# Eight token tiles of an attention output projection: fp32 products against three fp32r products, on one Trainium2 core

## The chip, the cores and the metric

The kernel runs on one core of one Trainium2 (trn2) chip. The metric is the device time of one launch in microseconds (us). The kernel before took 902.72 us, the median of three runs (902.1 to 905.22). The engines are TensorE (PE in the profile; PEld is its load of the stationary operand), VectorE (DVE), ScalarE (ACT), GpSimd (POOL) and SyncE (SP); SP, ACT and POOL also issue DMAs.

## The reference, cut to what matters

The input x has 2 batches of 1024 tokens of 512 numbers, 2048 tokens in all.

```
xn  = layernorm(x)
qkv = xn @ w_attn + b_attn                  # 16 heads of 32
q, k = rope(q), rope(k)
attn = softmax(causal(q @ k.T)) * 512**-0.5
o    = attn @ v                             # back to 2048 x 512
out  = x + (o @ w_proj + b_proj) + moe(xn)  # 8 experts, top 2
```

The change is about `o @ w_proj`: a product of 2048 x 512 by 512 x 512, and only about its first 1024 tokens (batch 0).

## The kernel before, in words

The kernel has three stages, and each is a block that ends only when all engines have done their part: `project_qkv` (layernorm, q, k, v, router), `attend` (attention and the output product of batch 0) and `experts` (the output product of batch 1, then the experts over 39 slot tiles).

**Attention.** Work goes in 16 rounds (`ROUNDS`), numbered n = 0 to 15. Round n handles one pair of heads of one batch, the set n mod 4. Each of the four sets has its own stack of queries, `q_st[i]`, and of keys, `k_st[i]`, of 128 partitions by 2048 fp32r numbers. Sets 0 and 1 belong to batch 0, sets 2 and 3 to batch 1. So `q_st[0]`, `k_st[0]`, `q_st[1]`, `k_st[1]` are last read in rounds 12 and 13, `q_st[2]` and `k_st[2]` in round 14, and only set 3 is used in round 15. A round has 12 steps (`NS`); a step has two score products (L1467), two exponentials on ACT (L1340) and two products with the values (L1487). In 8 steps of the 12, POOL sets the masked half of the probabilities to zero (L1285), and TensorE's products with the values wait for that (semaphore `masked`). The row maxima are computed a round and a half ahead (`LEAD` = 36 of 24 units per round): score products of their own on TensorE (L1444) and reductions on DVE (L1370, L1374). So DVE's part of the rounds ends in the middle of round 14.

**Scaling.** After every two rounds the sums of the exponentials of a "span" (one group of 8 heads of one batch: 8 spans, `SPANS`) go to memory and back through SP's queue: `load_totals` (L1178), DVE's reciprocal (`share`, L1392), `store_shares` (L1182), `spread_shares` (L1190), and then POOL multiplies that part of `o_t` (`scale_span`, L1270). The seventh span, the last of batch 0, is scaled in round 15. The eighth span belongs to batch 1; its `share` stands in DVE's program right after the first of the eight additions described next.

**The output product of batch 0** (`EARLY` = 8 tiles of 128 tokens). When its rounds are done, TensorE waits for the first seven spans (`scaled`) and for all banks, and then runs for each tile four fp32 products of 128 x 128 by 128 x 512, added up in one PSUM bank (L1529). The eight tiles use six banks in turn (`proj_banks`), so tiles 6 and 7 wait for DVE to be done with tiles 0 and 1 (`res_done`). DVE adds the residual (L1418) and SP stores the tile (L1220). POOL meanwhile adds the bias to the residual of the second half (`add_bias`, L1259, eight of them).

**The hand-over.** The block ends when SP has issued the last store and all engines are done. In `experts`, POOL then builds an identity matrix (L785, L787), TensorE waits for it and starts the output product of batch 1 (L990, the same fp32 form), and the expert tiles follow.

The fp32r form is already used elsewhere: `project_qkv` computes q and k as hi*hi + hi*lo + lo*hi (L535 to L537, 512 columns each), with a high part rounded to fp32r and a low part that is the difference. Differences of the same kind on DVE are L357 and L890; L351 is an addition of the same shape from SBUF to SBUF.

Of the kernel before, what the change touches and what calls it, by code (L numbers as in the profile page):

```python
# [18 lines left out]
ALU = mybir.AluOpType  # L19
# [3 lines left out]
P = 128  # L23
B, S, D = 2, 1024, 512
# [9 lines left out]
NG = H // HG  # L34
# [6 lines left out]
PAIR = 2  # L41
# [3 lines left out]
EARLY = S // P  # L45
# [4 lines left out]
def as_f32(ap):  # L50

    return ap.bitcast(F32)
# [946 lines left out]
def attend(nc, keep, scratch, x, w_proj, b_proj):  # L999
# [3 lines left out]
    ROUNDS = NG * SETS  # L1003
# [12 lines left out]
    NS = len(steps)  # L1016
# [9 lines left out]
    SPANS = NG * B  # L1026
# [24 lines left out]
    with ctx:  # L1051
        m = Memory(nc, ctx)
        q_st = [m.sbuf(f"q_stack{i}", [P, PAIR, S], F32R) for i in range(SETS)]
        k_st = [m.sbuf(f"k_stack{i}", [P, PAIR, S], F32R) for i in range(SETS)]
# [15 lines left out]
        o_t = keep["o_t"]  # L1070
# [5 lines left out]
        mb = [m.psum(f"maxima{r}", [P, CH]) for r in range(RING)]  # L1076

        proj_banks = scores_t + mb

        scattered, tags_in = m.sem("scattered"), m.sem("tags_in")  # L1080
        w_proj_in = m.sem("w_proj_in")
# [9 lines left out]
        st_full = m.sem("st_full")  # L1091
# [6 lines left out]
        scaled = m.sem("o_scaled")  # L1098
        bp_in, res_in, biased = m.sem("bp_early_in"), [m.sem(f"res_in{i}") for i in range(NT // 2)], m.sem("biased_early")
        proj_full, res_done = m.sem("proj_early_full"), m.sem("res_early_done")  # L1100
        acc_rows = scratch["acc"][0:T, :].rearrange("(a p) (g t) -> a p g t", p=P, t=P)
        QK_LOADS = 6
        OUTS = 2 * PAIR
# [256 lines left out]
        def _(dve):  # L1360
# [26 lines left out]
            def share(span):  # L1387

                dve.wait_ge(totals_in, 16 * (span + 1))
                if span:  # L1390
                    dve.wait_ge(shares_out, 16 * span)
                nc.vector.reciprocal(shares[:], totals[:]).then_inc(shares_done, 1)  # L1392

            def ahead(slot):

                if unit_at(slot) is not None:
                    n, u = unit_at(slot)
                    unit(n, u)
                    if u == NU - 1:
                        join(n)  # L1400
                if turn_at(slot - LOW_LAG) is not None:
                    row_low(turn_at(slot - LOW_LAG))
# [5 lines left out]
            for n in range(ROUNDS):  # L1408
                for u in range(NU):
                    ahead(n * NU + u)  # L1410
                    if u == (NB - 1) * PER - 1 and n % PAIRS == 0 and n:
                        share(n // PAIRS - 1)
                if n == 1:
                    route_owners(dve)
            for a in range(EARLY):
                dve.wait_ge(proj_full, a + 1)
                dve.wait_ge(biased, a + 1)
                nc.vector.tensor_tensor(o_t[:, :, a * P:(a + 1) * P], proj_banks[a % len(proj_banks)][:].rearrange("p (g t) -> p g t", t=P),  # L1418
                                        res[:, a, :].rearrange("p (g t) -> p g t", t=P), ALU.add).then_inc(res_done, 1)
                if a == 0:  # L1420
                    share(SPANS - 1)

        @block.tensor
        def _(pe):
# [83 lines left out]
            for n in range(ROUNDS):  # L1508
                for s in range(NB):
                    for x in range(BATCH * PAIR):  # L1510
                        k, h = (s + 1) * BATCH + x // PAIR, x % PAIR
# [13 lines left out]
            for a in range(EARLY):  # L1525
                if a >= len(proj_banks):
                    pe.wait_ge(res_done, a - len(proj_banks) + 1)
                for g in range(NG):
                    last = nc.tensor.matmul(proj_banks[a % len(proj_banks)][:], o_t[:, g, a * P:(a + 1) * P], keep["w_proj"][:, g, :],  # L1529
                                            start=(g == 0), stop=(g == NG - 1))  # L1530
                last.then_inc(proj_full, 1)


# [72 lines left out]
```

## Time and profile before

| what | value |
|---|---|
| median of the runs | 902.72 us |
| the profiled execution: its own time, its span | 906.29 us, 904.6 us |
| granted TensorE clock over the span | 0.954 |
| busy over the span: PE, DVE, ACT, POOL | 91%, 57%, 44%, 28% |
| output product of batch 0 on TensorE (L1529) | from 533.15 to 560.9 us |
| its records, additions on DVE | 64 records of 32 products, 8 additions |

The span is the time from the first to the last instruction of the profiled execution; 1.7 us lie around it. That execution took 3.6 us more than the median. Each fp32 product shows as two matmul records. A record's duration is longer than the distance between two starts, since products are pipelined: the distance between starts is what one costs in a row of many. The granted clock of 1.00 is 2.4 GHz and 0.50 is 1.2 GHz; values between are mixtures of the two over a stretch.

### The profile page before, as it was taken

What the parts mean: (1) busy time and instruction counts of PE and PEld (TensorE: products, weight loads), DVE (VectorE), ACT (ScalarE), POOL (GpSimd) and SP (SyncE); (2) the same over time, 40 slices, a digit from 0 to 9 for tenths busy, and PEclk for the clock granted to TensorE, in tenths of its full rate; (3) what the DMA queues carried; (4) which work ended last, traced back from release to release, by engine and by line L of the source; (5) the groups of instructions that cost most, each with busy time, mean ns of one, the idle gap of its engine ahead of it and who ended that gap; (6) DMA issues with size and microseconds to landing.
All of it is one profiled execution on the core that took longest, in us unless ns stands there. A gap on an engine that the chain in (4) does not pass through costs nothing. (4 is left out here: it accounts for less than half of the span.)

```text
span 904.6 us, 13761 instructions
## 1 busy us (share of the span) xinstructions
PE 820.4 (91%) x3973; PEld 559.8 (62%) x3974; DVE 515.3 (57%) x1334; ACT 394.8 (44%) x779; POOL 249.4 (28%) x314
## 2 busy tenths in 40 slices
PE   3889999569989999999999998979999999999990
PEld 3768989435445555555555443458778777787860
DVE  5992543395466667666666401166666666666640
ACT  3231231104445556555555630046666655556630
POOL 3782000134132424323233251002223223222220
PEclk9899999856899999999999999999999999999995
DMA  9386695894445755597671014843663664633327
GB/s 323 144 254 198 201 320 182 269 236 144 145 148 144 229 140 160 134 234 188 180 180 56 15 57 113 278 151 70 165 160 75 168 173 73 172 71 70 70 35 208
DMA packets 80477, 143.21 MB, mean 158 GB/s; under 512 B 16688, under 2 KB 30512, under 8 KB 80368
## 3 DMA queue, kind: packets, MB, share of 16 engines
q10 hardware_dynamic: 29056, 58.28, 23.8%
q1 hardware_dynamic: 43200, 65.72, 23.6%
q0 software_dynamic: 8176, 18.65, 9.8%
q8 instruction: 22, 0.36, 0.2%
q14 instruction: 23, 0.19, 0.1%
HBM read 81.21 MB, written 61.15 MB: 157 GB/s over the span
## 5 line engine op out<-in xcount | busy, mean ns | idle before, releaser
L1340 ACT ACTIVATE probs<-scores_t 128x512 f32<-128x512 f32 (+3 forms) x384 | 163.8, 492 | 148.7 <-PE scores_t L1467 136.9
L890 DVE TENSOR_TENSOR w_lo<-w,w_hi 128x704 fp32r<-128x704 f32 x156 | 131.7, 885 | 91.1 <-ACT w_hi L822 83.7
L1444 PE MATMUL maxima<-k_stack,q_stack 96*128 96x512 f32 (+3 forms) x384 | 142.2, 391 | 15.0 <-DMA q_stack<-qk_hi 9.0
L1487 PE MATMUL o_acc<-probs,v_ones 128*64 128x512 f32 (+3 forms) x768 | 149.9, 513 | 0.0
L1467 PE MATMUL scores_t<-q_stack,k_stack 98*128 98x512 f32 (+3 forms) x384 | 138.5, 386 | 7.2 <-DMA q_stack<-row_lo 5.1
L1374 DVE TENSOR_REDUCE mx<-maxima 128x1 f32<-128x512 f32 x128 | 88.2, 689 | 89.5 <-PE maxima L1444 89.3
L1370 DVE CUSTOM_DVE_ANT_0 masked_scores<-maxima,mask_m 128x128 f32<-128x128 f32 (+3 forms) x256 | 121.5, 485 | 23.8 <-PE maxima L1444 20.7
L822 ACT CAST w_hi<-w 128x704 fp32r x156 | 114.1, 783 | 34.2 <-issue 33.5
L935 PE MATMUL gu<-w_hi,rows_hi 128*128 128x352 f32 x312 | 119.7, 384 | 5.3 <-DVE rows_lo L883 4.0
L1467 PEld LDWEIGHTS scores_t<-q_stack,k_stack 98*128 98x128 f32 x384 | 73.6, 194 | 70.0 <-issue 42.7
L953 PE MATMUL down<-w,hidden_t 128*128 (+1 forms) x234 | 108.0, 597 | 0.8 <-DVE hidden_t L877 0.8
L936 PE MATMUL gu<-w_lo,rows_hi 128*128 128x352 f32 x312 | 101.5, 325 | 0.0
L937 PE MATMUL gu<-w_hi,rows_lo 128*128 128x352 f32 x312 | 101.3, 325 | 0.0
L1444 PEld LDWEIGHTS maxima<-k_stack,q_stack 96*128 96x128 f32 x384 | 77.5, 204 | 35.8 <-issue 9.5
L1285 POOL TENSOR_SCALAR_AFFINE_SELECT probs<-probs 128x256 f32<-128x256 f32 x120 | 48.4, 406 | 145.1 <-ACT probs L1340 143.5
L1487 PEld LDWEIGHTS o_acc<-probs,v_ones 128*64 128x64 f32 x768 | 47.8, 139 | 64.5 <-issue 39.6
L834 ACT ACTIVATE y<-down,tags 128x512 f32<-128x512 f32 x39 | 26.9, 689 | 107.7 <-PE down L953 58.7
L800 POOL COPY row_index<-tags 128x1 f32 (+1 forms) x39 | 8.7, 223 | 234.2 <-ACT y L834 173.3
L935 PEld LDWEIGHTS gu<-w_hi,rows_hi 128*128 128x128 f32 x312 | 59.1, 189 | 15.4 <-DVE w_lo L890 7.7
L801 POOL DMA_INDIRECT acc<-y,row_index x39 | 63.3, 1624 | 16.8 <-issue 15.4
L953 PEld LDWEIGHTS down<-w,hidden_t 128*128 128x128 f32 (+1 forms) x234 | 42.1, 190 | 39.8 <-issue 38.3
L280 ACT ACTIVATE st_hi<-bank,small 128x512 fp32r<-128x512 f32 x32 | 21.9, 687 | 101.8 <-PE bank L537 101.8
(158 smaller groups left out, 1168.9 us busy)
## 6 DMA issues: line engine op xcount, KB each, us to landing
w<-in_w_t SPq DMA_DIRECT2D x8, 1408.0 KB, 6.6
routed<-blank_row ACTq DMA_DIRECT2D x20, 514.0 KB, 6.5
rows<-routed ACTq DMA_DIRECT2D x39, 256.0 KB, 3.5
qk_hi<-st_hi SPq DMA_DIRECT2D x32, 256.0 KB, 4.7
qk_lo<-st_lo SPq DMA_DIRECT2D x32, 256.0 KB, 6.0
q_stack<-qk_hi ACTq DMA_DIRECT2D x32, 256.0 KB, 4.1
k_stack<-qk_hi ACTq DMA_DIRECT2D x26, 256.0 KB, 4.7
v_all<-o_t SPq DMA_DIRECT2D x4, 1536.0 KB, 5.7
```

The source lines that it names most:

```text
L822: nc.scalar.copy(w1_hi[r][:, k, :], w1_rows(slot, k)).then_inc(w1_hi_done, 1)
L890: nc.vector.tensor_tensor(w1_lo[r][:, k, :], w1_rows(slot, k), as_f32(w1_hi[r][:, k, :]), ALU.subtract).then_inc(w1_done, 1)
L935: nc.tensor.matmul(out, hi, w1_hi[r][:, k, cols], start=(k == 0), stop=False)
L936: nc.tensor.matmul(out, hi, w1_lo[r][:, k, cols], start=False, stop=False)
L937: last = nc.tensor.matmul(out, lo, w1_hi[r][:, k, cols], start=False, stop=(k == DK - 1))
L953: last = nc.tensor.matmul(down[r][:], hidden_t[r][0:n, k, :], w2[0:n, bass.ds(e, 1), k, :].rearrange("p o n -> p (o n)"), start=(k == 0), ...
L1340: nc.scalar.activation(probs[:, k % PR, h, 0:w], scores_t[e % RING][:, 0:w], ACT.Exp).then_inc(exp_done, 1)
L1370: nc.vector.tensor_tensor_reduce(out=masked_scores[bank][:, 0:w], in0=scores, in1=mask_m[:, CH - w:CH], scale=1.0, scalar=NEG, op0=ALU.add ...
L1374: nc.vector.tensor_reduce(to, scores, AX.X, ALU.max).then_inc(m_free, 1)
L1444: nc.tensor.matmul(mb[at % RING][:, 0:w], q_st[i][0:3 * HD, h, t * P:(t + 1) * P], k_st[i][0:3 * HD, h, c * CH:c * CH + w], start=True, st ...
L1467: last = nc.tensor.matmul(out[:, 0:w], k_st[i][0:STACK, h, j * P:(j + 1) * P], q_st[i][0:STACK, h, t0:t0 + w], start=True, stop=not diag)
L1487: last = nc.tensor.matmul(o_acc[c][2 * HD * h:2 * HD * (h + 1), CH - w:CH], v_st[i][:, j, h:h + 2, :].rearrange("p o d -> p (o d)"), probs ...
```

## The change

Each fp32 product of the eight tiles becomes three fp32r products, and DVE makes the four operands: the high and low part of `w_proj` (4 pieces of 512 columns) and the high and low part of `o_t` (8 tiles of 4 x 128 columns). The parts of `w_proj` go into `q_st[2]` and `k_st[2]`, as soon as all score products of rounds 0 to 14 are done (`st_full`). The parts of `o_t` go into the stacks of sets 0 and 1 (tile a into set a // 4, high in the query stack, low in the key stack), as soon as seven spans are scaled. All 24 new DVE instructions stand ahead of the eight additions in DVE's program. TensorE waits for each tile's low part, and for the four pieces of the weights.

```diff
+        wp_hi, wp_lo = (t[2][:].rearrange("p h (g n) -> p (h g) n", n=D) for t in (q_st, k_st))
+        def projected(stacks, a):
+            page = stacks[a // NG][:].rearrange("p h (x n) -> p (h x) n", n=D)
+            return page[:, a % NG, :]
...
+            def output_weights(g):
+                if g == 0:
+                    dve.wait_ge(w_proj_in, 16)
+                    dve.wait_ge(st_full, (ROUNDS - 1) * NS * PAIR)
+                nc.vector.tensor_copy(wp_hi[:, g, :], keep["w_proj"][:, g, :]).then_inc(wp_hi_done, 1)
+                dve.wait_ge(wp_hi_done, g + 1)
+                nc.vector.tensor_tensor(wp_lo[:, g, :], keep["w_proj"][:, g, :], as_f32(wp_hi[:, g, :]), ALU.subtract).then_inc(wp_done, 1)
+            def projected_parts(a):
+                tile = o_t[:, :, a * P:(a + 1) * P]
+                hi, lo = (projected(t, a).rearrange("p (g t) -> p g t", t=P) for t in (q_st, k_st))
+                if a == 0:
+                    dve.wait_ge(scaled, SPANS - 1)
+                nc.vector.tensor_copy(hi, tile).then_inc(o_hi_done, 1)
+                dve.wait_ge(o_hi_done, a + 1)
+                nc.vector.tensor_tensor(lo, tile, as_f32(hi), ALU.subtract).then_inc(o_done, 1)
+            for g in range(NG):
+                output_weights(g)
+            for a in range(EARLY):
+                projected_parts(a)
             for a in range(EARLY):
                 dve.wait_ge(proj_full, a + 1)
                 dve.wait_ge(biased, a + 1)
...
+                bank = proj_banks[a % len(proj_banks)]
+                pe.wait_ge(o_done, a + 1)
+                pe.wait_ge(wp_done, NG)
                 for g in range(NG):
-                    last = nc.tensor.matmul(proj_banks[a % len(proj_banks)][:], o_t[:, g, a * P:(a + 1) * P], keep["w_proj"][:, g, :],
-                                            start=(g == 0), stop=(g == NG - 1))
+                    hi, lo = (projected(t, a)[:, g * P:(g + 1) * P] for t in (q_st, k_st))
+                    nc.tensor.matmul(bank[:], hi, wp_hi[:, g, :], start=(g == 0), stop=False)
+                    nc.tensor.matmul(bank[:], hi, wp_lo[:, g, :], start=False, stop=False)
+                    last = nc.tensor.matmul(bank[:], lo, wp_hi[:, g, :], start=False, stop=(g == NG - 1))
                 last.then_inc(proj_full, 1)
```

## Rows read from the trace of the kernel before

**Rows 1.** Page, busy time of the engines and the chain that ended last.

```profile
PE 820.4 (91%) x3973; PEld 559.8 (62%) x3974; DVE 515.3 (57%) x1334; ACT 394.8 (44%) x779; POOL 249.4 (28%) x314
PE 34%; DVE 1%; issue 1%; POOL 0%; ACT 0%; ACTq 0%; DVEq 0%; POOLq 0%
```

**Rows 2.** Busy time by stretch; then granted clock, DMA share, GB/s.

```profile
core 0: us, PE busy (x) PEld busy (x) DVE busy (x) ACT busy (x) POOL busy (x), PEclk, DMA share, GB/s
88.20:93.75 5.55, 5.55 (x26) 4.46 (x24) 2.47 (x11) 1.49 (x3) 0.00 (x0) 1.00 1.07 267
533.15:560.90 27.75, 27.74 (x66) 12.09 (x64) 5.19 (x8) 0.58 (x1) 10.00 (x8) 1.00 0.31 92
560.90:563.50 2.60, 0.00 (x0) 0.00 (x0) 0.69 (x1) 0.00 (x0) 0.54 (x3) 1.00 0.26 74
591.70:595.70 4.00, 0.00 (x0) 0.00 (x0) 3.97 (x6) 1.85 (x4) 0.00 (x0) 1.00 0.80 279
595.70:600.00 4.30, 4.27 (x18) 4.20 (x19) 1.70 (x2) 1.96 (x4) 0.00 (x0) 0.60 0.21 63
```

**Rows 3.** VectorE in order of time, 508 to 563 us: start, duration, instruction, idle before.

```profile
511.07 0.33 DVE L1392 RECIPROCAL shares<-totals 128x32 f32<-128x32 f32 x1
536.89 0.69 DVE L1418 TENSOR_TENSOR o_t<-scores_t,x_rows 128x512 f32<-128x512 f32 x1 [25.50 <-PE scores_t L1529]
538.83 0.35 DVE L1392 RECIPROCAL shares<-totals 128x32 f32<-128x32 f32 x1 [1.25 <-DMA totals<-totals_all]
...
560.92 0.69 DVE L1418 TENSOR_TENSOR o_t<-scores_t,x_rows 128x512 f32<-128x512 f32 x1 [2.74 <-PE scores_t L1529]
```

**Rows 4.** TensorE in order of time, 88 to 94 us: first and last of 24 products.

```profile
88.20 0.40 PE L535 MATMUL bank<-xt_hi,w_hi 128*128 128x512 f32 x1
...
93.52 0.39 PE L537 MATMUL bank<-xt_hi,w_lo 128*128 128x512 f32 x1
```

**Rows 5.** TensorE in order of time, end of rounds 14 and 15.

```profile
512.51 0.56 PE L1467 MATMUL scores_t<-q_stack,k_stack 98*128 98x256 f32 x3
513.37 0.33 PE L1467 MATMUL scores_t<-q_stack,k_stack 98*128 98x128 f32 x1 [0.30 <-ACT probs L1340]
...
518.76 1.73 PE L1487 MATMUL o_acc<-probs,v_ones 128*64 128x512 f32 x8
...
530.85 2.37 PE L1487 MATMUL o_acc<-probs,v_ones 128*64 128x512 f32 x16
533.15 1.12 PE L1529 MATMUL scores_t<-w_proj,o_t 128*128 128x512 f32 x2
```

**Rows 6.** GpSimd in order of time, 516 to 563 us.

```profile
516.98 0.41 POOL L1285 TENSOR_SCALAR_AFFINE_SELECT probs<-probs 128x256 f32<-128x256 f32 x1 [2.49 <-ACT probs L1340]
517.74 0.41 POOL L1285 TENSOR_SCALAR_AFFINE_SELECT probs<-probs 128x256 f32<-128x256 f32 x1 [0.36 <-ACT probs L1340]
...
525.72 2.38 POOL L1270 TENSOR_TENSOR o_t<-o_t,share_rows 128x1024 f32<-128x1024 f32 x1 [6.10 <-DMA share_rows<-shares_all]
...
530.88 0.82 POOL L1285 TENSOR_SCALAR_AFFINE_SELECT probs<-probs 128x256 f32<-128x256 f32 x2 [1.72 <-ACT probs L1340]
531.67 9.13 POOL L1259 TENSOR_TENSOR x_rows<-x_rows,bp_early 128x512 f32<-128x512 f32 x8
544.69 2.35 POOL L1270 TENSOR_TENSOR o_t<-o_t,share_rows 128x1024 f32<-128x1024 f32 x1 [3.88 <-DMA share_rows<-shares_all]
562.81 0.21 POOL L785 MEMSET ident<- 128x128 f32 x1 [15.78 <-POOLq L1051]
```

**Rows 7.** Single lines: ns min/median/max, first and last start.

```profile
L435 DVE TENSOR_SCALAR x_rows<-x_rows,mean_var,rstd x2: 542/542/543, 12.6 to 13.1; 128x512 f32<-128x512 f32 x2
L357 DVE TENSOR_TENSOR w_lo<-w_raw,w_hi x8: 680/1090/1361, 27.7 to 46.6; 128x512 fp32r<-128x512 f32 x8
L226 POOL TENSOR_SCALAR x_rows<-x_rows,mean_var,rstd x12: 2070/2074/3512, 42.2 to 71.3; 128x512 f32<-128x512 f32 x12
```

**Rows 8.** SyncE's queue in order of time, 530 to 562 us.

```profile
542.41 19.75 SPq L1220 DMA_DIRECT2D acc<-o_t  x8
```

**Rows 9.** Groups by line, 513 to 542 us: TensorE's load for the products with the values.

```profile
L1487 PEld LDWEIGHTS o_acc<-probs,v_ones 128*64 128x64 f32 x64 | 4.0, 136 | 4.7 <-issue 2.9 <-POOL probs L1285 0.9 <-ACT probs L1340 0.3
```

More of the change, by code:

```diff
@@ L1100, in attend @@
         proj_full, res_done = m.sem("proj_early_full"), m.sem("res_early_done")
+        wp_hi_done, wp_done = m.sem("wp_early_hi_done"), m.sem("wp_early_done")
+        o_hi_done, o_done = m.sem("o_early_hi_done"), m.sem("o_early_done")
         acc_rows = scratch["acc"][0:T, :].rearrange("(a p) (g t) -> a p g t", p=P, t=P)
```

## The prediction, on record before the changed kernel ran

> **What bounds the kernel now.** I began with the page. TensorE is busy 91% of the span, and the chain that ended last lies almost wholly on TensorE [rows 1]. That chain begins only behind the last hand-over between blocks, so for the output product of batch 0 I read the stretches and the order of time instead. In the stretch from 533.15 to 560.90 us, TensorE is busy 27.74 of 27.75 us at a granted clock of 1.00, 2.4 GHz, while DVE has 5.19 us of work, ACT 0.58 and POOL 10.00 [rows 2]. No engine waits in TensorE's place: the tile's additions on DVE start at 536.89 and 560.92 us for the first and the last of eight, and each waits for TensorE [rows 3]. Seven intervals in 24.03 us make 3.433 us per tile, which is 0.858 us per fp32 product. Behind the last addition come its store on SP (issued by 542.41 + 19.75 = 562.16 us [rows 8]) and the hand-over: POOL starts the next block at 562.81 us [rows 6]. So what TensorE saves between 533 and 561 us moves all that follows, if nothing else becomes last there.
>
> **TensorE's part, the gain.** Each tile has 12 fp32r products of 512 columns in place of 4 fp32 ones. The nearest rows are the products of q and k, of the same shape and form: 24 of them start between 88.20 and 93.52 us, so 23 intervals make 0.2313 us each [rows 4], at a granted clock of 1.00 [rows 2]. A tile then takes 12 x 0.2313 = 2.776 us, 0.657 us less than 3.433. Eight tiles save 5.3 us. The loads of the stationary operand go from 64 records to 96 and hide under the products, as they do in the q and k stretch, where 24 loads take 4.46 of 5.55 us [rows 2]. The new waits between tiles cost nothing when they are already met: q and k have such waits between groups of 12 as well, and the distance does not grow there.
>
> By the Trainium skill (TensorE: Matmul & The Clock Gate, Back-to-back issue gap) an isolated product of 512 columns takes N / 2.4 + 2.5 ns, about 216 ns; the trace agrees for a record of the fp32 form (429 ns for two passes) and not for fp32r (231 ns). By the page the saving would be 6.7 us. I take the trace.
>
> **VectorE's part, the cost.** DVE is idle from 511.4 to 536.89 us, 25.5 us [rows 3]. Into this gap go 4 x (copy + difference) for the weights and the first of 8 x (copy + difference) for the tiles.
> - A difference of 128 x 512, SBUF to SBUF, is 680 ns at best and 1361 at most [rows 7].
> - A copy from SBUF to SBUF on DVE is in no row. The nearest is a one-source operation of 128 x 512, 542 ns; I take 0.54. The lower end is half of it, 0.27, the upper end is the difference's worst, 1.36 [rows 7].
> - With two short waits of some 0.03 us I take 1.28 us for a pair, with 0.98 and 2.72 as ends.
>
> The weights can start when the score products of round 14 are done, about 513.7 us [rows 5]; four pairs end at about 518.8 us, at the worst 524.6. That is before the seventh span is scaled, 525.72 + 2.38 = 528.1 us [rows 6], so the weights cost nothing. The eight tiles' parts start at 528.1 and end at 538.3 us undisturbed. TensorE wants tile a at 533.15 + 2.78 a; part a is there at 528.1 + 1.28 (a + 1), at the worst 528.1 + 2.72 (a + 1): 530.8 against 533.15 for the first, 549.9 against 552.6 for the last. TensorE never waits for parts within the bounds.
>
> **VectorE and GpSimd together.** From 531.67 us POOL has eight bias additions of 9.13 us in all [rows 6]. The trace shows that the two disturb each other: the difference goes from 680 to 1361 ns, POOL's operation from 2070 to 3512 [rows 7]. If the rest of the parts (about 6.6 us at 531.67) and the bias additions simply take turns, both are done at about 547 us; undisturbed 538. I take the middle, 543. By the Trainium skill (SBUF — State Buffer, Who interferes with whom) a VectorE instruction with two SBUF inputs, or a copy in its two-port mode, and a GpSimd instruction that reads SBUF take turns, one blocking the other wholly; by that rule it would be the 547, and the forecast stands at either.
>
> **What is queued behind the parts.** All eight additions and the last `share` wait behind them.
> - Tile 6 needs the bank of tile 0 at 533.15 + 6 x 2.78 = 549.8 us. The first addition ends 0.7 us behind the parts, at 543.7 (539.0 to 550.6). Cost 0, at the worst 0.8 us.
> - The last `share` ended at 539.18 us and POOL's last scaling began at 544.69, 5.5 us later, and took 2.35 [rows 3, 6]. Now `share` ends 1.1 us behind the parts, at 544.1, and the scaling at 552.0 us (549.9 gives 558.9). TensorE's own chain now ends with the last addition at 561.61 - 5.3 = 556.3 us. So the scaling is hidden with 4 us to spare, and is 2.6 us late at the very worst.
> - SP's stores start behind `spread_shares`, at some 547.5 instead of 542.41 us, and eight issues of about 0.5 us catch up before 556.3. The hand-over of some 1.2 us from the last addition to POOL stays.
>
> **The selects.** In rounds 14 and 15, ten of POOL's selects (L1285) fall in the time of the new DVE work. Two have little room: at 517.74 the end is 518.15 and the product with the values starts at 518.76 [rows 5, 6]; the two at 530.88 end at 531.70 and their products are the second half of a run from 530.85 to 533.2. TensorE's loads waited only 0.9 us for selects in all this stretch [rows 9]. A delay of one DVE instruction (0.54 to 0.68) costs at most some tenths. I take 0.2 us, near the lower end, because of those rooms; the ends are 0 and 14.4 (ten times 3512 - 2070 ns), and the upper one is rival 4.
>
> **Sum.** -5.3 + 0.2 = -5.1 us. The profiled execution would go from a span of 904.6 to 899.5 and from 906.3 to 901.2 us. It is 3.6 us above the median; the saving is a difference and holds for the median too: 902.7 - 5.1 = 897.6 us. A difference of about 0.3%, 2.7 us, is what a measurement here can tell from none.
>
> **Rivals.**
> 1. Products at the pass time of the fp32 rows: 0.2146 us each, gain 8 x (3.433 - 2.575) = 6.9, 896.0 us with the selects' 0.2. Against it stands every fp32r row. 0.06.
> 2. The last scaling becomes the end. It needs nearly every DVE instruction at 1.36 us. The end is 558.9, the gain 2.7, 900.0 us. Then TensorE stands still about 5 us at the hand-over. Before, 2.6 us of standing still left the granted clock at 1.00, and behind 4.0 us it was 0.60 for 4.3 us, a loss of 1.7 us [rows 2]; so up to 901.7. 0.08.
> 3. No gain: the change does not do what it says. If fp32r products out of these stacks go at 0.286 us or slower, three of them cost as much as one fp32 product, and the time stays at 902.7. For it: an operand that DVE has just written is read by a waiting TensorE. Against: q and k do that too, at 0.231. Also here belongs a gain that the expert block swallows; that block's loads start at the hand-over and move along with it. 0.07.
> 4. Slower: the selects. DVE runs its parts back to back, POOL gets in late each time, and TensorE's products with the values wait. It happens at 513.7 to 519 and 528.1 to 531.7 us. Ten selects at 1.44 us are 14.4 us: 902.7 - 5.3 + 14.4 = 911.8 us. It cancels the gain from 0.53 us of unabsorbed delay per select, and is visibly slower from 0.80. Against it: most selects have 1 to 2 us of room. 0.05.
>
> The forecast, parts and chain hidden, has 0.74. Rival 2 is half in "faster" and half in "same"; a little of the forecast goes to "same" for the spread of the runs. Faster 0.82, same 0.12, slower 0.06. The range takes in the forecast and rivals 1 and 2: 895.4 to 900.9 us.
>
> **What would show it.** In the profile after: 96 matmul records on TensorE in a stretch of about 22.3 us from 533.2 us, fp32r starts 0.231 us apart, granted clock 1.00; DVE's additions 2.78 us apart at the end; eight differences between 528.1 and some 543 us, between 0.68 and 1.36 us; POOL's bias additions stretched beyond 9.1 us; the last scaling ended by 552 us; the block's hand-over at about 557.7 instead of 562.81. Starts 0.286 us apart, a TensorE idle in the stretch, a hand-over that waits for POOL's scaling, or round 15 ending later than 533.4 would prove it wrong.

## The result, and the profile after

The changed kernel took 901.96 us, the median of 22 runs (895.79 to 910.98). The kernel before, run beside it, took 906.85 us (22 runs, 901.9 to 912.6, the three of the table above among them). The ratio is 0.9937, 95% interval 0.9918 to 0.9955: 5.7 us less, between 4.1 and 7.4. Here and below a median is of all runs, while a ratio and its interval leave out the runs that are over 1.5% above the fastest of the same kernel (two of the changed kernel's 22), so that the two medians differ by 4.9 us and the ratio says 5.7. The forecast was a saving of 5.1 us and a time of 897.6. The saving came as forecast and the time did not: it lies 4.4 us above the number and 1.1 us above the range. Both have to be explained.

The page of the kernel after, its first part and its chain, which answer to [rows 1]. The chain is still TensorE's; the 24 new instructions on DVE are 20 us more busy time.

```profile
span 898.8 us, 13858 instructions
PE 815.8 (91%) x4005; PEld 566.6 (63%) x4006; DVE 535.8 (60%) x1358; ACT 395.3 (44%) x779; POOL 253.7 (28%) x314
PE 34%; DVE 1%; issue 1%; POOL 0%; ACTq 0%; ACT 0%; DVEq 0%; POOLq 0%
```

Busy time by stretch in the kernel after, the counterpart of [rows 2]: the output products, the hand-over, the first 6 us behind it, TensorE's idle ahead of the expert tiles and the stretch behind that.

```profile
core 0: us, PE busy (x) PEld busy (x) DVE busy (x) ACT busy (x) POOL busy (x), PEclk, DMA share, GB/s
532.43:554.50 22.07, 22.05 (x98) 17.94 (x96) 16.19 (x17) 0.59 (x1) 13.14 (x9) 1.00 0.35 96
554.50:557.12 2.62, 0.00 (x1) 0.01 (x1) 0.69 (x1) 0.00 (x0) 0.56 (x3) 1.00 0.81 241
557.12:563.00 5.88, 5.88 (x14) 2.76 (x15) 0.69 (x1) 1.49 (x2) 0.08 (x1) 1.00 0.97 327
585.30:589.30 4.00, 0.00 (x0) 0.00 (x0) 3.97 (x6) 1.85 (x4) 0.00 (x0) 1.00 0.84 288
589.30:594.00 4.70, 4.67 (x20) 4.61 (x21) 1.69 (x2) 2.49 (x5) 0.00 (x0) 0.64 0.21 61
```

The first row is the gain: 22.07 us where 27.75 stood, so 5.68 us less, and TensorE is busy in all of it, as before. The hand-over is as long as it was (2.62 against 2.60 us). DVE has 16.19 us of work in the stretch where it had 5.19.

TensorE in order of time in the kernel after: the end of round 15, the first three and the last of the 96 products, the first product of the next block ([rows 4, 5] are the counterparts).

```profile
530.13 2.37 PE L1518 MATMUL o_acc<-probs,v_ones 128*64 128x512 f32 x16
532.43 0.50 PE L1564 MATMUL scores_t<-q_stack 128*128 128x512 f32 x1
532.77 0.40 PE L1565 MATMUL scores_t<-k_stack,q_stack 128*128 128x512 f32 x1
533.00 0.39 PE L1566 MATMUL scores_t<-q_stack,k_stack 128*128 128x512 f32 x1
...
554.10 0.39 PE L1566 MATMUL scores_t<-q_stack,k_stack 128*128 128x512 f32 x1
557.12 3.27 PE L990 MATMUL gu<-w_proj,o_t 128*128 128x512 f32 x7 [2.63 <-POOL ident L787]
```

95 intervals from 532.43 to 554.10 us make 0.2281 us, not 0.2313. No row in between shows an idle time ahead of a product, so no wait for parts or banks cost anything.

VectorE in order of time in the kernel after, where 25.5 us of idle stood [rows 3]: parts of the weights, parts of the tiles, additions.

```profile
513.09 0.54 DVE L1428 CAST q_stack<-w_proj 128x512 fp32r<-128x512 f32 x1 [2.40 <-PE scores_t L1498]
513.67 0.77 DVE L1430 TENSOR_TENSOR k_stack<-w_proj,q_stack 128x512 fp32r<-128x512 f32 x1
...
527.56 0.61 DVE L1438 CAST q_stack<-o_t 128x512 fp32r<-128x512 f32 x1 [9.59 <-POOL o_t L1278]
...
536.27 1.31 DVE L1438 CAST q_stack<-o_t 128x512 fp32r<-128x512 f32 x1
537.62 1.67 DVE L1440 TENSOR_TENSOR k_stack<-o_t,q_stack 128x512 fp32r<-128x512 f32 x1
539.21 1.32 DVE L1438 CAST q_stack<-o_t 128x512 fp32r<-128x512 f32 x1
...
543.49 0.69 DVE L1440 TENSOR_TENSOR k_stack<-o_t,q_stack 128x512 fp32r<-128x512 f32 x1
544.10 0.68 DVE L1449 TENSOR_TENSOR o_t<-scores_t,x_rows 128x512 f32<-128x512 f32 x1
544.70 0.34 DVE L1400 RECIPROCAL shares<-totals 128x32 f32<-128x32 f32 x1
...
554.52 0.69 DVE L1449 TENSOR_TENSOR o_t<-scores_t,x_rows 128x512 f32<-128x512 f32 x1 [2.03 <-PE scores_t L1566]
```

The last two additions still wait for TensorE (2.03 us of idle ahead of each), so DVE has caught up when it matters.

GpSimd in order of time in the kernel after ([rows 6]), and SyncE's stores ([rows 8]).

```profile
530.16 1.30 POOL L1293 TENSOR_SCALAR_AFFINE_SELECT probs<-probs 128x256 f32<-128x256 f32 x2 [1.71 <-ACT probs L1348]
531.43 11.73 POOL L1267 TENSOR_TENSOR x_rows<-x_rows,bp_early 128x512 f32<-128x512 f32 x8
550.59 2.40 POOL L1278 TENSOR_TENSOR o_t<-o_t,share_rows 128x1024 f32<-128x1024 f32 x1 [7.42 <-DMA share_rows<-shares_all]
556.41 0.21 POOL L785 MEMSET ident<- 128x128 f32 x1 [3.42 <-POOLq L1051]
```

```profile
548.27 7.48 SPq L1228 DMA_DIRECT2D acc<-o_t  x8
```

The next block starts 556.41 - 532.43 = 23.98 us behind the first output product, where it was 562.81 - 533.15 = 29.66: again 5.68 us. The row to keep in mind is the third: the last scaling ends at 552.99 us, and POOL's next instruction comes 3.42 us later. Before, 15.78 us lay between them, and nothing was to be learned from that.

**Where the 5.7 us show and where they do not.** Each time below is read between starts on TensorE. F is the first output product, N the first product of the next block, G the first product of the expert tiles. The clock is the granted one in the first 6 us behind N.

| profile of | F | F to N | N to G | G to end | span | clock |
|---|---|---|---|---|---|---|
| before | 533.15 | 30.37 | 32.21 | 308.87 | 904.6 | 1.00 |
| before_again | 531.90 | 30.37 | 33.90 | 309.43 | 905.6 | 0.72 |
| after | 532.43 | 24.69 | 32.21 | 309.47 | 898.8 | 1.00 |
| after_again | 535.78 | 24.68 | 35.25 | 309.89 | 905.6 | 0.50 |
| after_third | 528.83 | 24.68 | 33.91 | 309.18 | 896.6 | 0.72 |

The rows of N and G in the kernel before, TensorE in order of time:

```profile
563.52 24.30 PE L990 MATMUL gu<-w_proj,o_t 128*128 128x512 f32 x56 [2.63 <-POOL ident L787]
...
595.73 0.43 PE L935 MATMUL gu<-w_hi,rows_hi 128*128 128x352 f32 x1 [4.04 <-DVE rows_lo L883]
```

"again" and "third" are the same kernels, profiled anew beside the experiments below. F to N is the same to 0.01 us in each kernel, and 5.69 us apart. Everything else moves from run to run: F by 7 us, N to G by 3 us. So one profile's span says little on a change of 5 us, and this stretch says nearly all.

### The profile page after: what moved, and what is told of

Its sections match the earlier page's. It is cut to its first block and busy times, and to the rows that moved or that the text cites. A ratio compares the mean times of both kernels' runs of the same rounds, so it can differ in the third digit from the quotient of the medians.

```text
span 898.8 us, 13858 instructions
## 1 busy us (share of the span) xinstructions
PE 815.8 (91%) x4005; PEld 566.6 (63%) x4006; DVE 535.8 (60%) x1358; ACT 395.3 (44%) x779; POOL 253.7 (28%) x314
## 5 line engine op out<-in xcount | busy, mean ns | idle before, releaser
L280 ACT ACTIVATE st_hi<-bank,small 128x512 fp32r<-128x512 f32 x32 | 21.9, 687 | 102.2 <-PE bank L537 102.2
```

## The experiments

Three questions. Is the gain the products' form, and is DVE's new work free? How much room was there at the hand-over? Is there more to be had, in the second half? The sessions' medians of the kernel before were 908.55 (23 runs; the first four experiments), 908.49 (27 runs), 908.45 (17 runs) and 908.11 us (17 runs). Lines given in diffs are against the changed kernel.

**parts_only: the parts without the products.** DVE makes all parts and TensorE waits for them, and the products stay in fp32.

```diff
                 for g in range(NG):
-                    hi, lo = (projected(t, a)[:, g * P:(g + 1) * P] for t in (q_st, k_st))
-                    nc.tensor.matmul(bank[:], hi, wp_hi[:, g, :], start=(g == 0), stop=False)
...
+                    last = nc.tensor.matmul(bank[:], o_t[:, g, a * P:(a + 1) * P], keep["w_proj"][:, g, :],
+                                            start=(g == 0), stop=(g == NG - 1))
```

> VectorE makes all parts as in the changed kernel and TensorE waits for them, but the products stay the four fp32 ones per tile of the kernel before. Theory (the gain is TensorE's pitch alone, the parts are hidden): from the first output product to the first product of the next block 30.4 us as before, ratio to before 1.000 within 0.002. Rival (the parts cost something in rounds 14 and 15, through the selects, or through the share behind them): round 15 ends later, or the hand-over comes after 30.4 us, ratio 1.002 or more.

Measured: 909.62 us (12 runs), ratio 0.9996 (0.9972 to 1.0021). F to N is 30.37 us, the kernel before to the last digit. DVE's 24 instructions, and the stretched bias additions and selects on POOL, cost nothing that can be seen; the 5.69 us are the products' alone. With fp32 products POOL's scaling had 9.27 us before the next block, so how close the parts come to costing something in the changed kernel is the next experiments' question.

**one_term: TensorE's work nearly taken away.** DVE still makes all parts, but the kernel leaves out the two products with a low part and keeps hi*hi alone.

```diff
-                    hi, lo = (projected(t, a)[:, g * P:(g + 1) * P] for t in (q_st, k_st))
-                    nc.tensor.matmul(bank[:], hi, wp_hi[:, g, :], start=(g == 0), stop=False)
-                    nc.tensor.matmul(bank[:], hi, wp_lo[:, g, :], start=False, stop=False)
-                    last = nc.tensor.matmul(bank[:], lo, wp_hi[:, g, :], start=False, stop=(g == NG - 1))
+                    hi = projected(q_st, a)[:, g * P:(g + 1) * P]
+                    last = nc.tensor.matmul(bank[:], hi, wp_hi[:, g, :], start=(g == 0), stop=(g == NG - 1))
```

> Leaves out the two products with a low part (hi*hi alone), so TensorE's work in the eight tiles falls from 21.9 to some 7.3 us; all parts are still made. Theory (next in line behind TensorE are the parts, the eighth share and its scaling, which ended at 553.0 us in the changed kernel): the next block's first product comes 22.0 us after the first output product, against 24.7 in the changed kernel, only 2.7 us earlier for 14.6 us less work; TensorE then stands still some 7 us, its granted clock falls and some 2 us of that go again: ratio to before 0.991 to 0.995. Rival (nothing else is near): some 14 us less, ratio 0.978.

Measured: 900.54 us, ratio 0.9877 (0.9831 to 0.9923, four runs). Two thirds of TensorE's products in this stretch are gone, some 14.6 us, and F to N falls from 24.69 only to 24.40 us; 22.0 were expected, because the expectation let the next block follow the scaling (20.56 us behind F in the kernel after) by some 1.4 us. The ratio lies below the 0.991 to 0.995 expected, and further below 1 than the profile's stretches bear out (F to G is 58.24 us, against 62.58 and 64.27 in the kernel before): it rests on few runs. TensorE in order of time in one_term: it waits for parts, for a bank, and then 8.33 us for the next block.

```profile
531.25 3.01 PE L1564 MATMUL scores_t<-q_stack 128*128 128x512 f32 x12
534.10 2.27 PE L1564 MATMUL maxima<-q_stack 128*128 128x512 f32 x8
538.07 1.73 PE L1564 MATMUL maxima<-q_stack 128*128 128x512 f32 x4 [1.70 <-DVE k_stack L1440]
543.54 3.78 PE L1564 MATMUL scores_t<-q_stack 128*128 128x512 f32 x8 [3.74 <-DVE o_t L1449]
555.65 1.22 PE L990 MATMUL gu<-w_proj,o_t 128*128 128x512 f32 x1 [8.33 <-POOL ident L787]
```

GpSimd in order of time in one_term shows what it waited for.

```profile
549.41 2.34 POOL L1278 TENSOR_TENSOR o_t<-o_t,share_rows 128x1024 f32<-128x1024 f32 x1 [7.53 <-DMA share_rows<-shares_all]
554.94 0.21 POOL L785 MEMSET ident<- 128x128 f32 x1 [3.19 <-POOLq L1051]
```

The scaling ends at 551.75 us and the next block's first instruction on POOL starts 3.19 us later. So there is a floor: with the parts as they are, the end of the block cannot come earlier than 3.19 us behind this scaling, whatever TensorE does. It is not SP: its last store is issued by 553.51 us, 1.43 us ahead of the next block, where 0.66 us were enough in the kernel after. Nor is it DVE, whose last addition ends at 548.04 us. The changed kernel is 0.3 us above the floor. What fills the 3.19 us the profile does not show.

**adds_early: GpSimd out of DVE's way.** The eight bias additions a = 8 to 15 move into the rounds.

```diff
+            ADDS = [(0, 1), (2, 3), (4, 5, 6), (7, 8, 9), (10, 11, 12), (13, 14, 15)]
...
-                    if k == TPC and BIAS_ROUND <= n < BIAS_ROUND + EARLY // 2:
-                        add_bias(2 * (n - BIAS_ROUND))
-                        add_bias(2 * (n - BIAS_ROUND) + 1)
-            for a in range(EARLY, NT):
-                add_bias(a)
+                    if k == TPC and n >= BIAS_ROUND:
+                        for a in ADDS[n - BIAS_ROUND]:
+                            add_bias(a)
```

> GpSimd's bias additions of the second half are moved into rounds 12 to 15, so that none runs beside the parts of o_t. Theory (two-input and copy instructions of VectorE take turns with GpSimd): all copies of o_t go back to 0.41 us and all differences to 0.69 us, and the parts end near 537 instead of 544 us; the time does not change, 24.7 us from the first output product to the next block, ratio 0.992 to 0.996, since the parts were hidden. Rival (the parts' late end costs something at the hand-over): 0.3 us or more faster than the changed kernel there. Third possibility: the moved additions delay selects in rounds 14 and 15, and these rounds end later.

Measured: 901.19 us, ratio 0.9904 (0.9873 to 0.9934). F to N is 24.70 us, so nothing is gained at the hand-over. From the last row of the maxima (510.68 us) to F are 24.76 us, as in the kernels before and after, so the moved additions did not lengthen the end of the rounds either. VectorE in order of time in adds_early, one pair of the undisturbed ones and the last part's end:

```profile
536.56 0.42 DVE L1437 CAST q_stack<-o_t 128x512 fp32r<-128x512 f32 x1
537.02 0.69 DVE L1439 TENSOR_TENSOR k_stack<-o_t,q_stack 128x512 fp32r<-128x512 f32 x1
537.62 0.42 DVE L1437 CAST q_stack<-o_t 128x512 fp32r<-128x512 f32 x1
...
539.14 0.69 DVE L1439 TENSOR_TENSOR k_stack<-o_t,q_stack 128x512 fp32r<-128x512 f32 x1
...
557.54 0.69 DVE L1448 TENSOR_TENSOR o_t<-scores_t,x_rows 128x512 f32<-128x512 f32 x1 [2.03 <-PE scores_t L1565]
```

and GpSimd in order of time in the same kernel:

```profile
546.90 2.40 POOL L1279 TENSOR_TENSOR o_t<-o_t,share_rows 128x1024 f32<-128x1024 f32 x1 [12.32 <-DMA share_rows<-shares_all]
559.43 0.21 POOL L785 MEMSET ident<- 128x128 f32 x1 [10.13 <-POOLq L1051]
```

A pair costs 1.06 us here, from the start of a copy to the start of the next (536.56 to 537.62), against 2.94 us beside the bias additions in the kernel after (536.27 to 539.21). The parts end 4.4 us behind F instead of 11.8, and the scaling has 10.13 us before the next block. The next block comes 1.20 us behind DVE's last addition (558.23 to 559.43), exactly as before (561.61 to 562.81) and after (555.21 to 556.41). So two distances from last work to next block are known: 1.20 us behind DVE's, at least 3.19 us behind POOL's. In the kernel after, 552.99 + 3.19 = 556.18 us against 555.21 + 1.20 = 556.41: the scaling had 0.23 us of room. In after_again, below, the gap was 3.27 us, so that it had 0.08.

**parts_twice: the suspected cost doubled.** The parts of the tiles are made twice, and TensorE waits for the second.

```diff
-                nc.vector.tensor_copy(hi, tile).then_inc(o_hi_done, 1)
-                dve.wait_ge(o_hi_done, a + 1)
-                nc.vector.tensor_tensor(lo, tile, as_f32(hi), ALU.subtract).then_inc(o_done, 1)
+                for turn in range(2):
+                    nc.vector.tensor_copy(hi, tile).then_inc(o_hi_done, 1)
+                    dve.wait_ge(o_hi_done, 2 * a + turn + 1)
+                    nc.vector.tensor_tensor(lo, tile, as_f32(hi), ALU.subtract).then_inc(o_done, 1)
+                    dve.wait_ge(o_done, 2 * a + turn + 1)
...
-                pe.wait_ge(o_done, a + 1)
+                pe.wait_ge(o_done, 2 * a + 2)
```

> VectorE makes the parts of each tile of o_t twice (the same values), 16 instructions more, before TensorE may use them. Theory (TensorE bound only as long as the parts and the share behind them end early; the room is some 3 us): the parts end near 552.5 us, TensorE waits before tiles 2, 3 and 6, the eighth scaling ends near 561.5, and the next block's first product comes 30.4 us after the first output product, the gain is gone: ratio 0.999 to 1.003. Rival (VectorE's work is well hidden, much room): ratio stays at 0.994 to 0.996.

Measured: 912.67 us, ratio 1.0031 (0.9997 to 1.0065), F to N 34.60 us: 9.9 more than the kernel after, where 30.4 us were expected. The scaling ended 30.70 us behind F, where the expectation had 29.1 (561.5 us in the kernel after's times), and N came 3.90 us behind it, where the expectation had 1.3: the same slip as in one_term. GpSimd in order of time in parts_twice:

```profile
556.54 2.34 POOL L1278 TENSOR_TENSOR o_t<-o_t,share_rows 128x1024 f32<-128x1024 f32 x1 [17.97 <-DMA share_rows<-shares_all]
562.08 0.21 POOL L785 MEMSET ident<- 128x128 f32 x1 [3.19 <-POOLq L1051]
```

3.19 us again, the same distance with the scaling 7 us later. Here the prediction's rival 2 is real, and dearer than priced: TensorE stands still for 6.41 us ahead of the next block.

**before_again and after_again: the same two kernels once more,** to see what moves between profiles of one kernel.

> The kernel before, unaltered, as if it were a change: ratio 1.000, with an interval that shows how finely these comparisons resolve (some 0.003). The stretch from the first output product to the next block is 30.4 us again, while the time at which that product starts differs by microseconds from 533.15, since the first half of the attention runs at a granted clock that differs from run to run.

> The changed kernel once more, unaltered, against the kernel before in the same session. Theory (the saving is a fixed stretch of TensorE's work, the absolute time drifts with the session): ratio 0.9937 within 0.003, that is 5 to 6 us less, whatever the median of the kernel before is this time; from the first output product to the next block 24.7 us again. Rival (the saving itself varies, for the room at the hand-over is only some 0.2 us): that stretch is 25.5 us or more in this profile.

Measured: before_again 908.98 us, ratio to the kernel before 1.001 (0.9984 to 1.0037); after_again 899.61 us, 0.9905 (0.9868 to 0.9943), where 0.9937 within 0.003 was expected. Busy time by stretch in after_again, the same three stretches as of the kernel after:

```profile
535.78:557.85 22.07, 22.05 (x98) 17.93 (x96) 16.24 (x17) 0.59 (x1) 13.19 (x9) 1.00 0.35 95
557.85:560.46 2.61, 0.00 (x0) 0.00 (x0) 0.69 (x1) 0.00 (x0) 0.56 (x3) 0.87 0.87 251
560.46:566.50 6.04, 6.04 (x7) 2.52 (x8) 0.00 (x0) 1.49 (x2) 0.08 (x1) 0.50 0.97 328
```

The same idle of 2.6 us left the granted clock at 1.00 in one profile and at 0.50 (1.2 GHz) in the other; the record is that 6.04 us of TensorE work then hold 7 matmul records instead of 14. It costs 3.0 us of N to G. With it at 1.00, 0.72 and 0.50 N to G is 32.2, 33.9 and 35.3 us. The kernel before shows 1.00 and 0.72 too, and so does the kernel after, so those two levels come without the change; 0.50 behind this idle was seen only once, in after_again. Nor does the length of the idle settle it: behind 8.33 us in one_term the clock was 0.72 and N to G 33.84 us, behind 6.41 us in parts_twice 0.57 and 34.75.

**late_too, late_adds: the other half as well.** The second half of the output product (`experts`, L990) in three fp32r products, with the high parts made by ACT and the low parts by DVE at the block's start; late_adds has the edit of adds_early on top.

```diff
+            part_high(0)
+            for g in range(NG):
+                nc.scalar.copy(pw(0, g), wp[:, g, :]).then_inc(pw_hi_done, 1)
+            part_high(1)
...
+            part_low(0)
+            for g in range(NG):
+                dve.wait_ge(pw_hi_done, g + 1)
+                nc.vector.tensor_tensor(pw(1, g), wp[:, g, :], as_f32(pw(0, g)), ALU.subtract).then_inc(pw_done, 1)
...
-                    last = nc.tensor.matmul(gu[a % 2][a // 2 % 2][:], o_t[:, g, at * P:(at + 1) * P], wp[:, g, :],
-                                            start=(g == 0), stop=(g == NG - 1))
+                    if a == 0:
+                        pe.wait_ge(pw_done, g + 1)
+                    hi, lo = (part(t, a)[:, g, :] for t in (0, 1))
+                    nc.tensor.matmul(bank[:], hi, pw(0, g), start=(g == 0), stop=False)
+                    nc.tensor.matmul(bank[:], hi, pw(1, g), start=False, stop=False)
+                    last = nc.tensor.matmul(bank[:], lo, pw(0, g), start=False, stop=(g == NG - 1))
```

> The changed kernel with the output product of the second half (L990) in three fp32r products too: high parts of the weights and of the tiles by ScalarE, low parts by VectorE, in buffers that the first expert tile needs only later. Theory (every tile of output products is worth 0.69 us on TensorE while the parts are hidden): eight tiles save 5.6 us, of which some 2.5 us are lost at the start of the block, where the parts of the weights and of tile 0 are made in sight: 2.5 to 3.5 us faster than the changed kernel, ratio to before 0.989 to 0.992. Rival (TensorE's longer idle at the start of the block lowers its granted clock, as after the 4.0 us of idle before): a first stretch at 1.2 GHz eats most of it, ratio 0.992 to 0.995.

> The same, and the bias additions of the second half on GpSimd moved into rounds 12 to 15, so that the eighth scaling ends some 4 us earlier (it ended 3.4 us before the next block in the changed kernel, and 3.2 us is the least seen). Theory (that scaling was just hidden): the time is that of the kernel with both halves in fp32r, within 0.2%. Rival (it was at times the last): 0.2 to 0.5% less than that kernel.

Measured: 900.83 us, ratio 0.9922 (0.9892 to 0.9952), and 901.79 us, 0.9935 (0.9902 to 0.9968); the two are alike within their intervals, as the theory of late_adds had it, and neither is shown to be faster than the changed kernel. F to N is 27.20 us in both, 2.5 longer than in the kernel after, and N to G 29.6 and 29.5. TensorE in order of time in late_too:

```profile
559.07 0.76 PE L1036 MATMUL gu<-w_hi,rows_hi 128*128 128x512 f32 x1 [5.10 <-DVE w_lo L945]
```

It stands still for 5.10 us, for the weights' low parts. Behind N the products save some 4 us (29.6 against the 33.9 us of most profiles; 2.6 against the 32.2 at a clock of 1.00, while here it was 0.63), and ahead of N the parts give 2.5 of them back.

**late_kept, after_third: the weights' parts kept.** Both halves again, and the weights' parts stay in a buffer from the first half to the second, so that the second needs only those of its first tiles. `w_proj` comes in four loads in round 15, and the parts share the space of `st_hi` and `st_lo` of the first block.

```diff
-        wp_hi, wp_lo = (t[2][:].rearrange("p h (g n) -> p (h g) n", n=D) for t in (q_st, k_st))
+        wp_hi, wp_lo = keep["wp_hi"], keep["wp_lo"]
+        raw = masked_scores + [mask_m]
...
+                    if n == ROUNDS - 1 and k < NG:
+                        if k == 0:
+                            act.wait_ge(m_free, ROUNDS * NU)
+                        act.dma_start(raw[k][:], w_proj[k * P:(k + 1) * P, :]).then_inc(w_proj_in, 16)
```

> Both halves in fp32r, but the parts of the weights are kept from the attention block (w_proj is loaded in round 15 into the maxima's buffers), so that the second half waits only for the parts of its first tile. Theory (what made the first version of both halves no faster was 2.5 us of parts in sight at the start of the block, plus a first stretch at 1.2 GHz): the stretch from the first output product to the next block's first product is 25.4 us (27.2 in that version, 24.7 in the changed kernel), and from there to the first product of the expert tiles 27 us at a full granted clock, up to 29 with a fallen one (32.2 in the changed kernel); 3 to 5 us faster than the changed kernel, ratio to before 0.986 to 0.990. Rival (the expert block's first tile is set by its weights and ScalarE's casts, not by TensorE): the gap before the expert tiles grows by what the products save, ratio 0.991 to 0.994.

> The changed kernel unaltered, in the same session as the version above, to compare the two on one chip: ratio to before 0.9925 within 0.003.

Measured: late_kept 900.86 us, ratio 0.9893 (0.9845 to 0.9942, six runs), and the changed kernel beside it 902.3 us, 0.993 (0.9905 to 0.9956). F to N is 26.80 us, where 25.4 was expected, and N to G 30.33, where 27 to 29 was, with the clock at 0.52 in the first 6 us behind N. The forecast of 3 to 5 us over the changed kernel is not borne out.

**late_kept_adds, late_kept_again.** Is it POOL's scaling that makes late_kept's hand-over long? The edit of adds_early on late_kept, beside late_kept itself.

> Like late_kept (both halves of the output product in three fp32r products, the weights' parts kept for the second half), and GpSimd's eight bias additions a = 8 to 15 moved into rounds 12 to 15. It asks whether GpSimd's last scaling, the last to end at the block's end in late_kept (ended 551.63 us, GpSimd's next block 3.19 us later), is what separates its 26.80 us from first output product to first product of the next block from what TensorE needs. Theory (the 3.2 us behind GpSimd's last instruction ended last): the scaling then ends some 4 us earlier, the last wait ahead of the next block is one for VectorE or SyncE, the stretch is 25.4 us, that is 1.4 us shorter than late_kept's, and the ratio lies 0.0015 below that of late_kept_again. Rival (what ended last is VectorE's parts of the second half's first tile): the stretch stays at 26.8 and the ratios agree within their intervals.

> The same kernel as late_kept, a second look beside late_kept_adds. Expected: the stretch from the first output product to the next block's first product 26.80 us again, within 0.1, whatever the level; the stretch from there to the first expert tile 30.3 if the granted clock falls to 0.50 for the same 5.7 us around the hand-over as in late_kept, 27.5 to 28.5 if it stays at 1.00, as it did there in two profiles of the other kernels (32.21 us against 33.9); ratio to the kernel before 0.986 to 0.993. If the ratio comes out above 0.993, the late half's parts bring nothing that can be measured beside the change under study.

Measured: 902.0 us, ratio 0.9932 (0.99 to 0.9963), and 901.79 us, 0.9928 (0.9888 to 0.9968). GpSimd in order of time, late_kept_again first:

```profile
548.37 2.40 POOL L1317 TENSOR_TENSOR o_t<-o_t,share_rows 128x1024 f32<-128x1024 f32 x1 [9.48 <-DMA share_rows<-shares_all]
553.96 0.21 POOL L800 MEMSET ident<- 128x128 f32 x1 [3.19 <-POOLq L1089]
```

and late_kept_adds:

```profile
544.01 2.39 POOL L1318 TENSOR_TENSOR o_t<-o_t,share_rows 128x1024 f32<-128x1024 f32 x1 [12.95 <-DMA share_rows<-shares_all]
556.52 0.21 POOL L800 MEMSET ident<- 128x128 f32 x1 [10.12 <-POOLq L1089]
```

From F, 528.47 and 531.93 us, to the next block on POOL are 25.49 and 24.59 us: the mechanism is there and was worth 0.9 us, not 1.4. Of the 0.7 us by which late_kept_adds' F to N, 26.09 us, lies above the 25.4 expected, 0.6 are TensorE's: its 96 products start over 22.27 us (531.93 to 554.20), where they took 21.67 in the kernel after. F to N is 26.99 and 26.09 us (26.80 within 0.1 was expected of the first). TensorE's idle fell from 4.33 to 3.43 us, and here the clock stayed at 1.00, so N to G is 27.74 us against 30.23. That profile's F to G is 53.83 us, the shortest of all, 3.1 below the kernel after's shortest. The timed runs do not show it: the two ratios differ by 0.0004, in the wrong direction, and all five measurements with both halves in fp32r (0.9893 to 0.9935) lie where the changed kernel lies (0.9905 to 0.9937). G to end is 309.8 to 310.6 us in them against 309.2 to 309.9 in the changed kernel's profiles; why it grows was not tested. No version was shown to beat the changed kernel.

## Why the prediction was right, and where it was wrong

**The level was wrong, and it alone put the time outside the range.** The step that failed is this sentence under "Sum": "It is 3.6 us above the median; the saving is a difference and holds for the median too: 902.7 - 5.1 = 897.6 us." The saving does hold. But the median was one of three runs, and the profiled execution's 906.3 us was set aside as the odd one, where it was the typical one: 19 further runs of the same kernel have a median of 907.1 us, and those of the four later sessions lie from 908.1 to 908.6. Of the 4.4 us by which the forecast of 897.6 was low, 4.1 are this level (906.85 - 902.72); the rest is that the medians differ by 4.9 us and not 5.1. The prediction had both numbers in hand. From the profiled execution it reads 906.3 - 5.1 = 901.2 us, against 901.96 measured. That this single run would be the typical one could not be known beforehand: what could be known is that four times from 902.1 to 906.3 leave the level open by some us. What the level goes with shows in the runs: the time of the changed kernel's 22 runs goes against their mean granted clock with a correlation of -0.92, from 911 us at 0.941 to 896 us at 0.960. The clocks of the three first runs are not on record. Only 4 of the 19 further runs lie below the highest of the three, so whether the three were a lucky draw or had another level stays open. Three runs of a quantity that spreads over 11 us could not fix the level to better than some 3 us (an estimate from the standard deviation of the 22, 3.4 us), and the range left no room for that.

**TensorE's pitch: right mechanism, the saving 0.4 us larger.** 0.2313 us per product (from start to start) was taken, 0.2281 came. 96 products make 21.9 instead of 22.2 us; the stretch shrank by 5.68 us where 5.3 was forecast. The Trainium skill (TensorE: Matmul & The Clock Gate, Back-to-back issue gap) gives some 216 ns for an isolated product. The trace lies between the page and the q and k rows, and nearer to the rows: rival 1 did not happen. In the kernels that keep the weights' parts in another buffer the same products go at 0.234 us (the 96 of late_kept_adds from 531.93 to 554.20), so where the operands lie may have a part in it; that was not tested.

**TensorE never waited for parts: right.** The tile parts ended at 544.18 us for a forecast of 543. F itself came 0.7 us earlier than in the profile before, so the better measure is behind F: 11.75 us for a forecast of 9.85, still inside the 16.8 (549.9 - 533.15) of the worst case.

**DVE's prices: the terms were off both ways and cancelled.** Alone, a copy took 0.41 to 0.42 us for the 0.54 taken, a difference 0.69 for 0.68, so a pair 1.06 for 1.28. Beside POOL's bias additions the pair took 2.94 us, longer than the 2.72 that the prediction had as its worst. One pair there holds two POOL additions' turns: 1.31 - 0.41 and 1.67 - 0.69 us are 0.90 and 0.98 us of waiting, close to one addition's own 9.13 / 8 = 1.14 us [rows 6]. POOL's eight went from 9.13 to 11.73 us. From 531.43 us on the two engines' own work is 4 x 1.06 + 0.69 = 4.9 and 9.13 us, 14.1 together, and it was over in 12.75 us. The Trainium skill (SBUF — State Buffer, Who interferes with whom) has such instructions take turns, one blocking the other wholly; by that the end would be, as an estimate, 545.5 us; the trace had 544.18. That is near the rule, with 1.3 us of the two engines' work side by side after all, and far from the 536.4 us of no interference.

**The selects: right that they hardly matter.** 0.2 us was taken. In round 15 two selects took 1.30 us for 0.82 [rows 6], and TensorE's loads waited less for selects than the 0.9 us of [rows 9]. Groups by line of the kernel after, 512.3 to 532.4 us:

```profile
L1518 PEld LDWEIGHTS o_acc<-probs,v_ones 128*64 128x64 f32 x64 | 4.0, 136 | 4.7 <-issue 2.9 <-POOL probs L1293 0.6 <-ACT probs L1348 0.6
```

From the last row of the maxima (L1380, L1388 after: start at 508.40 and 507.69 us) to F are 24.75 and 24.74 us. Rival 4 is excluded.

**The last scaling: the largest error of mechanism, and it cost nothing by luck.** "So the scaling is hidden with 4 us to spare": it ended at 552.99 us, where 552.0 was forecast, and its room was 0.23 us, where 4.3 was forecast. The prediction set the scaling's end (552.0) against the end of the last addition (556.3) as if both were followed by the same 1.2 us. They are not: at least 3.19 us follow POOL's scaling (one_term, parts_twice, late_kept, late_kept_again), and 1.20 us follow DVE's addition. That difference took 2.0 us of the 4.3. The scaling ended 20.56 us behind F where 18.85 was forecast, which took 1.7, and the last addition ended 22.78 us behind F where 23.15 was, which took 0.4. Rival 2 was priced by the same slip: its bound of 558.9 us would have meant a hand-over at 562.1 us, just before the 562.81 of the kernel before, and so a gain of 0.7 us and not 2.7. parts_twice shows the case: its scaling ended 30.70 us behind F (528.18 to 558.88) and its next block began 33.90 us behind F, 4.2 us later than in the kernel before.

**The hand-over moved as forecast.** 557.7 - 533.15 = 24.55 us behind F was forecast, 23.98 came. The 2.6 us of idle were said to leave the clock at 1.00 because they had [rows 2]; in after_again it fell to 0.50 behind the same idle. One profile of one stretch was taken to hold for all.

Shown: the form of the products is the gain (parts_only), the parts are free while POOL's scaling ends 3.2 us ahead of the block (one_term, adds_early, parts_twice). Not shown: why the pitch is 0.228 us, what fills the 3.19 us behind POOL's scaling, why the chip grants a lower clock in one run than in another, and why the first three runs were lower than the others.

## What to carry to other kernels

Take the level of a prediction from all times at hand, the profiled execution's included, and give the range the spread of single runs when only a few are known: the difference can be right to 0.6 us and the time still 4 us off. Idle time on an engine ahead of a block's end is not room until it is set against what follows that engine's last instruction; ask for each engine how long that took. An operand that is split once and used for many products is cheap beside TensorE's saving, and where the split stands in the order is what matters: late_too lost at the start of a block more than half of what the same products saved.

## What the runs showed of the hardware that was not expected

- Behind POOL's last instruction of the block, a 128 x 1024 multiplication, its next block began 3.19 us later in one_term, parts_twice, late_kept and late_kept_again, to 0.01 us; behind DVE's last addition it was 1.20 us in the kernels before and after, adds_early and late_kept_adds.
- A copy with rounding from fp32 to fp32r, SBUF to SBUF, 128 x 512, took 0.41 us on DVE, a subtraction of the same size 0.69. Beside POOL's additions they took 1.31 and 1.67 us (in parts_twice, with other starts, 1.39 and 1.46): from start to start a pair stays at 2.92 to 2.94 us, and which of the two waits longer changes.
- After the same idle of 2.6 us on TensorE the granted clock of the next 6 us was 1.00, 0.72 or 0.50, run by run, worth 0, 1.7 and 3.0 us. Behind 8.33 us of idle it was 0.72, no lower than behind 2.6.
